# Self-loops of the gate's graph added at the node instead of as edges, and narrower look-ups in the sort

## Chip, cores and metric

One core of a Trainium2 chip runs the whole program, two layers of a graph network, in one launch. The metric is the device time of the launch in microseconds (us).

## What is computed

The reference is two layers over 3125 nodes of 256 values; each has a graph part over 53125 edges, a mixer and an expert layer. The change touches the last expert layer, whose gate is a graph attention over edges of its own: 32768 random pairs between nodes 0 to M-1, M being the number of nodes, and one loop for each node. In the kernel as in the reference (here cut):

```
h = (x_flat @ W_gat).reshape(M, HEADS, NUM_EXPERTS)
loops = jnp.arange(M)
src = concatenate([edge_index[0], loops])
dst = concatenate([edge_index[1], loops])
a_src = (h * att_src).sum(-1)
a_dst = (h * att_dst).sum(-1)
e = leaky_relu(a_src[src] + a_dst[dst], negative_slope=0.2)
e_max = segment_max(e, dst)
ee = exp(e - e_max[dst])
denom = segment_sum(ee, dst)
alpha = ee / (denom[dst] + 1e-16)
agg = segment_sum(h[src] * alpha[:, :, None], dst)
scores = layernorm(agg + b_gat).mean over heads
w = softmax of the two largest of 4 scores
out = sum over experts of w * (gelu(x @ W1 + b1) @ W2 + b2)
```

HEADS is 4 and NUM_EXPERTS 4, so `h` has 16 values a node.

## The kernel before

The program is a row of blocks. In a block each engine has its own list of instructions and waits on semaphores; at its end all engines wait for each other. Nodes stand in 25 blocks of 128. There is no scheduler: what an engine does next is the order written in its function.

**The gate's edges.** They arrive unsorted. `sort_and_route` (L1603) sorts them by destination, for later stages, in the middle of the program. The 32768 pairs fill 256 columns of 128 lanes, the loops 25 more, and 7 columns of fillers bring C2 to 288, 36 turns of U = 8 columns. A destination is split in a low digit (128 values) and a high digit (`so_hi`, NH = 26 values). The **count phase** writes one-hot rows of the low digit (L1912, VectorE) and multiplies them with the high digit's (L1764, TensorE). The **place phase** finds the place of each pair. In one turn: TensorE looks up the start of the pair's node in a table split in two parts (`look`, L1804, in two halves of four matmuls, 52 columns wide: both parts side by side), turns one-hots (`turn_low`, L1782), compares all lanes (`compare`, L1793) and counts equals of lower order (`rank`, L1813, 8 matmuls of 26 columns that add onto the look-ups); VectorE masks the comparison (`order`, L1984), splits the starts (`begin` L1972, `divide` L1977), and in `finish` multiplies the look-ups with the high one-hot (L1988, the pick), reduces (L1993) and casts them (L1995); ScalarE copies (L1867, L1874). In the program's order the first half of a turn's look stands ahead of the compare that the next `order` needs, and waits for the pick of the turn before last, since both use one PSUM tile (`so_g`).

**Scatters.** GpSimd then writes each pair to its place in a table in memory, 128 at a time, one instruction a column (class `Scatter` L2011, L2025), 281 columns. They are spread over stages: 48 in the place phase itself, at most one a turn up to turn 25 and then spread evenly over what is left (`upto_turn`, L1719, each waiting for the turn's cast), beside the routed rows of the first layer's experts; 192 in `experts0` (24 an expert, held back by `pace` to where TensorE is); 16 in `return0`, 25 in `gram1`. `experts0` runs 8 experts: TensorE's two matmul groups (L1465, L1474), a bias on VectorE (L1521) and stores issued by ScalarE (L1497). At the end of `gram1` VectorE works on a row of sums (L2269). 

**The gate.** `build_steps` (in `combine1`) cuts the sorted edges at blocks of nodes: T2 = C2 + NB - 1 = 312 steps, 39 turns. `gate_rows` (L2632) computes 20 values a node, h and a_src, into a table `h_tab`, and a_dst in three bf16 parts in `d_parts`. `gate_scores` (L2817) gathers 128 rows of `h_tab` a step on GpSimd (L2850), ring of four turns; TensorE spreads the destinations (L2889), multiplies the one-hot with `d_parts` (`fetch`, L2899); VectorE reduces the three parts and adds (L2927 to L2932). Behind this TensorE runs the last layer's first experts: each unit a block of nodes by one expert, a hidden half (L2774, `gs_x_h`) and an output half (L2784, `gs_x_y`), 160 such halves' groups spread evenly over the turns, with ScalarE's activation (L2807) and VectorE's bias (L2814) between. `segment_softmax` (L338) turns scores into exponentials of score less the segment's maximum, by scans, in a transposed layout: TensorE transposes into `m2_bank` (L395), VectorE masks (L460) and copies back (L465). Expert blocks run beside it. `gate_sums` (L2959) sums the exponentials and weighted rows by destination: rows cut in three bf16 parts (slices by ScalarE, L3016 and L3017, differences by VectorE, L3040 and L3041), in three chunks of 104 steps, one-hots by VectorE (L3048) and eight matmuls a turn (L3003); 12 expert blocks run between them, and the slices of the next chunk follow ScalarE's activations by the table `SLICED`. `top_two` (L3082) divides, adds the bias, normalises and picks; `experts1` (L3150) runs the rest.

The tile names in rows and orders: `so_` sort, `gs_` scores, `m_` and `m2_` softmax, `gu_` sums, `x_` and `x1_` experts.

## Time and profile before

| | us |
|---|---|
| median of 3 runs | 2887.47 (2885.08 to 2895.32) |
| the profiled execution, its time | 2890.44 |
| its span, first to last instruction | 2888.5 |
| busy TensorE / VectorE / GpSimd / ScalarE | 2220.0 / 1962.4 / 1644.1 / 1402.7 |
| mean granted TensorE clock | .859 |

Each stage's length is set by the engine that ends it. So a total of busy time (TensorE 77%) says little; a stage has to be read by itself, by the busy time of its engines in a stretch of the time axis, and its end by the timeline. In the rows below, PE is TensorE's matmuls, PEld its weight loads, DVE VectorE, ACT ScalarE, POOL GpSimd, SP SyncE; a q behind the name is the engine issuing a DMA. In a row of the timeline the brackets say how long the engine was idle before, and which instruction it waited for.

### The profile page before, as it was taken

The numbers are of one execution on the slowest core, as the hardware profiler recorded it, in microseconds if no ns is written. First come the engines' busy times: TensorE is split into PE (matmuls) and PEld (weight loads), VectorE is DVE, ScalarE is ACT, GpSimd is POOL, SyncE is SP. The second block draws the span as 40 slices with busy tenths as digits, with TensorE's granted clock in tenths as the row PEclk, the third lists the DMA queues.
The fourth block names the chain that finished last, engine by engine and source line by source line (L and its number), as shares of the span: only waits on it lengthen the run. The fifth ranks groups of instructions, "written<-read, shape, count | busy, mean of one in ns | idle before, by whom it ended". The sixth has DMA issues, their size and how long they took to land. (4 is left out here: it accounts for less than half of the span.)

```text
span 2888.5 us, 41571 instructions
## 1 busy us (share of the span) xinstructions
PE 2220.0 (77%) x11092; PEld 1493.3 (52%) x11092; DVE 1962.4 (68%) x4014; ACT 1402.7 (49%) x4464; POOL 1644.1 (57%) x1754
## 2 busy tenths in 40 slices
PE   6996777777777755779974587777787798888785
PEld 3553555555555555656632333333335777777664
DVE  4565999999999888810138799999996322222586
ACT  2221666666666544411133598999994422222242
POOL 2645766666665203567776777777774277777000
PEclk9998888888888855589986799999998699999898
DMA  3214767667665021224322333333331311111005
GB/s 107 57 48 133 212 194 208 201 200 202 201 207 164 1 61 55 66 64 128 99 65 88 87 105 103 104 104 105 103 105 29 73 39 39 31 38 34 14 1 190
DMA packets 170395, 293.24 MB, mean 102 GB/s; under 512 B 56092, under 2 KB 104737, under 8 KB 170174
## 3 DMA queue, kind: packets, MB, share of 16 engines
q0 software_dynamic: 79344, 187.14, 23.8%
q1 hardware_dynamic: 81672, 87.12, 9.7%
q10 hardware_dynamic: 9158, 16.33, 1.6%
q8 instruction: 102, 1.67, 0.2%
q14 instruction: 119, 0.97, 0.1%
HBM read 253.68 MB, written 36.78 MB: 101 GB/s over the span
## 5 line engine op out<-in xcount | busy, mean ns | idle before, releaser
L957 POOL DMA_INDIRECT at_kv<-kv_tab,e_src x440 | 433.8, 986 | 254.0 <-PE at_a L1079 139.1
L2447 PE MATMUL cv_ps<-cv_msg,cv_hot 128*128 128x512 f32 x880 | 421.1, 614 | 125.4 <-DVE acc L2509 83.6
L2434 POOL DMA_INDIRECT cv_x<-x_tab,e_src x440 | 425.6, 967 | 137.3 <-issue 92.3
L2850 POOL DMA_INDIRECT gs_h<-h_tab,fc_q x312 | 294.4, 943 | 161.0 <-issue 93.6
L2465 ACT ACTIVATE cv_msg<-cv_x,factors 128x64 f32<-128x64 f32 x1320 | 357.6, 335 | 0.0
L2025 POOL DMA_INDIRECT pairs<-gating_pair,gating_place x281 | 275.5, 980 | 138.4 <-issue 70.1
L2447 PEld LDWEIGHTS cv_ps<-cv_msg,cv_hot 128*128 128x128 f32 x880 | 158.9, 192 | 349.9 <-ACT cv_msg L2465 177.1
L2509 DVE TENSOR_TENSOR acc<-acc,cv_ps 128x256 f32 x880 | 307.0, 413 | 6.8 <-PE cv_ps L2447 5.2
L1079 PE MATMUL at_a<-at_kv,at_hot_e 128*128 128x264 f32 x880 | 255.6, 420 | 13.4 <-ACT at_hot_e L1006 9.2
L1054 PE MATMUL at_q<-q_parts,at_hot_n 128*128 x1320 | 227.2, 328 | 44.6 <-DVE at_kv L1151 21.9
L2807 ACT ACTIVATE gs_x_hid<-gs_x_h,x_b 128x128 f32<-128x128 f32 x320 | 91.2, 368 | 302.1 <-PE gs_x_h L2774 293.3
L2462 ACT ACTIVATE cv_msg<-cv_x,factors 128x256 f32<-128x256 f32 x440 | 218.3, 496 | 26.2 <-DMA cv_x<-x_tab,e_src 26.1
L2784 PE MATMUL gs_x_y<-x_w,gs_x_hid 128*128 128x256 f32 x640 | 170.0, 416 | 49.6 <-DVE gs_y L2814 49.1
L1054 PEld LDWEIGHTS at_q<-q_parts,at_hot_n 128*128 128x128 bf16 x1320 | 147.0, 113 | 114.6 <-issue 63.5
L1079 PEld LDWEIGHTS at_a<-at_kv,at_hot_e 128*128 128x128 f32 x880 | 165.3, 209 | 48.0 <-ACT at_hot_e L1006 19.2
L1016 ACT ACTIVATE at_kv<-at_kv 128x32 f32<-128x32 f32 x864 | 185.6, 306 | 0.0
L1180 DVE TENSOR_TENSOR acc<-acc,at_a 128x528 f32 x220 | 154.1, 701 | 41.6 <-PE at_a L1079 34.5
L2927 DVE TENSOR_REDUCE gs_as_dst<-gs_d 128x32 f32<-128x96 f32 x39 | 10.0, 258 | 251.6 <-DMA gs_h<-h_tab,fc_q 251.6
L2784 PEld LDWEIGHTS gs_x_y<-x_w,gs_x_hid 128*128 128x128 f32 x640 | 127.4, 208 | 71.3 <-issue 43.7
L2774 PE MATMUL gs_x_h<-xnT,x_w 128*128 128x128 f32 x1280 | 161.6, 283 | 0.0
L2774 PEld LDWEIGHTS gs_x_h<-xnT,x_w 128*128 128x128 f32 x1280 | 158.5, 199 | 2.7
L1151 DVE TENSOR_TENSOR at_kv<-at_kv,at_q 128x512 f32<-128x512 f32 x220 | 147.3, 681 | 14.8 <-DVE at_ends L1253 5.8
(548 smaller groups left out, 4347.2 us busy)
## 6 DMA issues: line engine op xcount, KB each, us to landing
x_space<-in_L_ffn_w SPq DMA_DIRECT2D x16, 1024.0 KB, 6.8
at_rel_row<-e_rel_rows SPq DMA_DIRECT2D x55, 256.0 KB, 4.5
experts_out<-gs_y ACTq DMA_DIRECT2D x20, 512.0 KB, 2.7
x_y<-experts_out SPq DMA_DIRECT2D x20, 512.0 KB, 7.0
at_kv<-kv_tab,e_src POOLq DMA_INDIRECT x440, 3.9
cv_x<-x_tab,e_src POOLq DMA_INDIRECT x440, 2.7
kv_tab<-p_qkv SPq DMA_DIRECT2D x25, 256.0 KB, 2.0
gs_h<-h_tab,fc_q POOLq DMA_INDIRECT x312, 2.4
```

Source lines behind the costliest of these rows:

```text
L957: nc.gpsimd.indirect_dma_start(out=kv[:, t % (RING * Q4), 0:2 * D], out_offset=None, in_=kv_tab, in_offset=bass.IndirectOffsetOnAxis(ap=e. ...
L1054: ins = nc.tensor.matmul(ps_q[dd % 3][:, u, :], hot_n[:, t // Q4 % NHOT, t % Q4 * P:(t % Q4 + 1) * P], q_parts[:, ds(b, 1), n, :].rearrang ...
L1079: nc.tensor.matmul(to, hot_e[:, t // Q4 % NEDGE, t % Q4, :], kv[:, t % (RING * Q4), D:2 * D + H1], start=(u == 0), stop=(u == 1), skip_gro ...
L2025: nc.gpsimd.indirect_dma_start(out=pairs, out_offset=bass.IndirectOffsetOnAxis(ap=place_i[:, c:c + 1], axis=0), in_=pair[:, c, :], in_offs ...
L2434: nc.gpsimd.indirect_dma_start(out=xg[:, i % RT, u, :], out_offset=None, in_=x_tab, in_offset=bass.IndirectOffsetOnAxis(ap=e.src[:, t:t + ...
L2447: nc.tensor.matmul(ps[u % R][:, :], hot[:, i % 2, u, :], msg[:, i % 2, u, :], start=True, stop=True).then_inc(summed, 1)
L2462: nc.scalar.activation(parts[:, 0], xg[:, i % RT, u, :].rearrange("p (r i) -> p r i", i=M), ACT.Copy, scale=factor[:, t:t + 1, 0])
L2465: ins = nc.scalar.activation(parts[:, 1, 1 + m], xg[:, i % RT, u, 0:M], ACT.Copy, scale=factor[:, t:t + 1, 1 + m])
L2509: v.tensor_tensor(row, row, ps[u % R][:, n * D:(n + 1) * D], ALU.add).then_inc(added, 1)
L2774: ins = self.nc.tensor.matmul(self.ps_h[e % 2][:, f * P:(f + 1) * P], self.x1.w1[:, e, c, f * P:(f + 1) * P], self.xnT[:, c, b * P:(b + 1) ...
L2784: ins = self.nc.tensor.matmul(self.ps_y[e % 2][:, 0:D], self.hid[:, e % 2, f, :], self.x1.w2[:, e, f, :], start=(f == 0), stop=(f == FX // ...
L2850: nc.gpsimd.indirect_dma_start(out=hg[:, i % RT, u, :], out_offset=None, in_=h_tab, in_offset=bass.IndirectOffsetOnAxis(ap=e.src[:, i * U ...
```

## The change

The loops are no edges any more. C2 is 256 columns (32 turns), T2 280 (35 turns). The node's own score is computed in `gate_rows` and kept behind a_dst in `d_parts` (24 values a fetch for 12); each edge's score is taken less it. The softmax then takes the larger of the segment's maximum and 0, and gives a second set of values, the exponential of minus that maximum, at the first edge of each segment: the loop's own weight. `gate_sums` adds both (24 columns for 20, 72 a matmul for 60), and `top_two` adds the own term times the node's h. A node with no edge has the weight 1. `gate_rows` keeps h of all blocks. `bank_row` holds the PSUM column where a step's block starts, as 7 blocks of 72 columns fill a bank of 512.

In the sort the two parts of the look-up and the rank are added up in the same 26 columns, so the look is 8 matmuls of 26 columns a half where it was 4 of 52, and the pick and its reduction take 208 elements for 416. The DMA of the fillers and the operations that prepared the loop pairs go. Scatters: 48 in the sort as before, 176 in experts0, 16 in return0, 16 in gram1.

The core of the diff; the pieces, in order, are of the constants, `sort_and_route`, `segment_softmax` (VectorE), `gate_rows`, `gate_scores` (VectorE), `gate_sums` and `top_two`:

```diff
-C2 = (CG + NB + U - 1) // U * U
+C2 = CG
...
-RETURN_SCATTER = C2 // U - 6
+RETURN_SCATTER = C2 // U - 4
...
-                        ins = nc.tensor.matmul(looked(h)[:, u, :, :].rearrange("p a n -> p (a n)"), lo_t[:, h, u, :],
-                                               part[:, h, u, :, :].rearrange("p a n -> p (a n)"), start=(u == 0), stop=False, skip_group_check=True)
+                        for a in range(2):
+                            ins = nc.tensor.matmul(looked(h)[:, u, :], lo_t[:, h, u, :], part[:, h, u, a, :], start=(u == 0 and a == 0),
+                                                   stop=False, skip_group_check=True)
...
-                    v.tensor_tensor(pick[:, :, :, :], looked(i % 2),
-                                    wide(hi[:, i * U:(i + 1) * U, :].unsqueeze(2), [P, U, 2, NH]), ALU.mult).then_inc(picked, 1)
+                    v.tensor_tensor(pick[:, :, :], looked(i % 2), hi[:, i * U:(i + 1) * U, :], ALU.mult).then_inc(picked, 1)
...
+                v.tensor_scalar(b[:, :, :, :], b[:, :, :, :], 0.0, None, ALU.max).then_inc(topped, 1)
+                dve.wait_ge(topped, 1)
                 v.tensor_tensor(x[:, :, :, :], x[:, :, :, :], b[:, :, :, :], ALU.subtract).then_inc(expd, 1)
                 keeps((1, 0), (1, 1))
+                dve.wait_ge(faded, 1)
+                for g in range(groups):
+                    ins = v.scalar_tensor_tensor(out=f[:, g], in0=wide(starts[:, g, :].unsqueeze(1), [P, heads, P]), scalar=0.0, in1=f[:, g],
+                                                 op0=ALU.is_lt, op1=ALU.mult)
+                ins.then_inc(firsts, 1)
                 dve.wait_ge(gone, 1)
...
+                c.link(v.tensor_tensor(own[:, :, :], h[:, :, 16:GW], as_dst[:, :, 0:H2], ALU.add))
+                c.link(v.scalar_tensor_tensor(out=as_dst[:, :, H2:2 * H2], in0=own[:, :, :], scalar=0.2, in1=own[:, :, :],
+                                              op0=ALU.mult, op1=ALU.max))
...
+                    v.tensor_tensor(score[:, i * U:(i + 1) * U, 0:H2], raw[:, :, :], as_dst[:, :, H2:2 * H2], ALU.subtract).then_inc(chain, 1)
...
-    CT = 13
+    CT = 9
-    SLICED = {1: (1, 0), 2: (1, 1), 3: (1, 2), 6: (2, 0), 7: (2, 1), 8: (2, 2)}
-    assert chunks == 3
+    SLICED = {3 * (q - 1) + n: (q, n) for q in range(1, chunks) for n in range(3)}
...
                     q, x = i // CT + 1, i % CT
                     if q < chunks:
-                        if x == 3:
+                        if x == 1:
                             weigh(q)
-                        elif x in (6, 9):
-                            dve.wait_ge(left, 3 * q + x // 3 - 1)
-                            leave(q, x // 3 - 2)
+                        elif x in (3, 6):
+                            dve.wait_ge(left, 3 * q + x // 3)
+                            leave(q, x // 3 - 1)
...
-                c.link(v.tensor_scalar(q[:, 0], acc[:, :, 16:20], 1e-16, None, ALU.add))
+                own, of_edges, total = acc[:, :, 20:24], acc[:, :, 16:20], q[:, 0]
+                c.link(v.tensor_tensor(total, of_edges, own, ALU.add))
+                c.link(v.scalar_tensor_tensor(out=q[:, 2], in0=total, scalar=0.0, in1=own, op0=ALU.is_equal, op1=ALU.add))
+                v.tensor_tensor(t[:, 1].rearrange("p b (h e) -> p b h e", e=NX), h[:, :, 0:16].rearrange("p b (h e) -> p b h e", e=NX),
+                                wide(q[:, 2].unsqueeze(3), [P, NB, H2, NX]), ALU.mult)
+                c.link(v.scalar_tensor_tensor(out=total, in0=q[:, 2], scalar=1e-16, in1=of_edges, op0=ALU.add, op1=ALU.add))
+                c.link(v.tensor_tensor(t[:, 0], acc[:, :, 0:16], t[:, 1], ALU.add))
```

In the place loop, TensorE's list of one turn, before (`so_s` is the comparison, `so_t` the turned one-hots, `so_g` the look-ups and ranks; a number behind the name is the buffer):

```order
L1804 MATMUL so_g1<-so_part,ef_h 128x52 x4
L1782 MATMUL so_t0<-ident_h,x0_space 128x128 x4
L1793 MATMUL so_s1<-ef_h 128x128 x4
L1804 MATMUL so_g1<-so_part,ef_h 128x52 x4
L1782 MATMUL so_t1<-ident_h,x0_space 128x128 x4
L1813 MATMUL so_g0<-so_hi,ef_h 128x26 x8
L1793 MATMUL so_s0<-ef_h 128x128 x4
```

and after:

```order
L1815 MATMUL so_g1<-so_part,ef_h 128x26 x8
L1792 MATMUL so_t0<-ident_h,x0_space 128x128 x4
L1803 MATMUL so_s1<-ef_h 128x128 x4
L1815 MATMUL so_g1<-so_part,ef_h 128x26 x8
L1792 MATMUL so_t1<-ident_h,x0_space 128x128 x4
L1824 MATMUL so_g0<-so_hi,ef_h 128x26 x8
L1803 MATMUL so_s0<-ef_h 128x128 x4
```

The order is the same; each look has 8 narrow matmuls where it had 4.

At the end of the softmax, TensorE's list before (`m2_x` holds the exponentials, `m2_x_h` and `m2_x_y` are an expert's halves):

```order
L395 MATMUL m2_bank0<-ident,m2_x 128x128 x4
L395 MATMUL m2_bank1<-ident,m2_x 128x128 x4
L395 MATMUL m2_bank2<-ident,m2_x 128x128 x4
L2774 MATMUL m2_x_h1<-xnT,x1_w1 128x128 x8
L2784 MATMUL m2_x_y0<-x1_w2,m2_x_hid 128x256 x4
L2784 MATMUL m2_x_y1<-x1_w2,m2_x_hid 128x256 x4
```

and after, with `m2_f` the second set and four banks used in a ring:

```order
L398 MATMUL m2_bank3<-ident,m2_f 128x128 x4
L398 MATMUL m2_bank0<-ident,m2_f 128x128 x4
L398 MATMUL m2_bank1<-ident,m2_f 128x128 x4
L398 MATMUL m2_bank2<-ident,m2_x 128x128 x4
L398 MATMUL m2_bank3<-ident,m2_x 128x128 x4
L398 MATMUL m2_bank0<-ident,m2_x 128x128 x4
L2778 MATMUL m2_x_h1<-xnT,x1_w1 128x128 x8
L2788 MATMUL m2_x_y0<-x1_w2,m2_x_hid 128x256 x4
L2788 MATMUL m2_x_y1<-x1_w2,m2_x_hid 128x256 x4
```

Six groups of transposes stand ahead of the next expert's hidden half where three did.

In `gate_sums`, the end of ScalarE's list before (`gu_part` are slices, `gu_x_hid` an expert's activations):

```order
L2807 ACTIVATE gu_x_hid<-gu_x_h0,x1_b1 128x128 x4
L2807 ACTIVATE gu_x_hid<-gu_x_h1,x1_b1 128x128 x4
L2807 ACTIVATE gu_x_hid<-gu_x_h0,x1_b1 128x128 x4
L3016 ACTIVATE gu_part<-gate_edge_rows 128x104x16
L3017 ACTIVATE gu_part<-score2 128x104x4
L2807 ACTIVATE gu_x_hid<-gu_x_h1,x1_b1 128x128 x4
L3016 ACTIVATE gu_part<-gate_edge_rows 128x104x16
L3017 ACTIVATE gu_part<-score2 128x104x4
L2807 ACTIVATE gu_x_hid<-gu_x_h0,x1_b1 128x128 x4
L3016 ACTIVATE gu_part<-gate_edge_rows 128x104x16
L3017 ACTIVATE gu_part<-score2 128x104x4
L2807 ACTIVATE gu_x_hid<-gu_x_h1,x1_b1 128x128 x4
```

and after:

```order
L3045 ACTIVATE gu_part<-gate_edge_rows 128x72x16
L3046 ACTIVATE gu_part<-score2 128x72x8
L2811 ACTIVATE gu_x_hid<-gu_x_h0,x1_b1 128x128 x4
L3045 ACTIVATE gu_part<-gate_edge_rows 128x64x16
L3046 ACTIVATE gu_part<-score2 128x64x8
L2811 ACTIVATE gu_x_hid<-gu_x_h1,x1_b1 128x128 x4
L3045 ACTIVATE gu_part<-gate_edge_rows 128x64x16
L3046 ACTIVATE gu_part<-score2 128x64x8
L2811 ACTIVATE gu_x_hid<-gu_x_h0,x1_b1 128x128 x4
L3045 ACTIVATE gu_part<-gate_edge_rows 128x64x16
L3046 ACTIVATE gu_part<-score2 128x64x8
L2811 ACTIVATE gu_x_hid<-gu_x_h1,x1_b1 128x128 x4
```

Slices now follow the activations up to the ninth, and the last ones have 64 steps.

## Rows read from the trace of the kernel before

**Rows 1.** busy us of PE, PEld, DVE, ACT, POOL, granted clock, DMA share, GB/s by stretch
```profile
1107.00:1235.00 128.00, 90.50 (x1146) 79.74 (x1144) 108.86 (x214) 60.58 (x130) 69.60 (x72) 0.51 0.23 67
2248.00:2285.00 37.00, 30.75 (x152) 29.84 (x152) 8.81 (x64) 22.42 (x51) 0.00 (x0) 0.50 0.51 125
2285.00:2685.00 400.00, 346.69 (x2304) 294.69 (x2305) 104.04 (x274) 91.89 (x321) 294.35 (x312) 0.92 0.17 35
```

**Rows 2.** the page's groups, the gate's gathers: busy, mean ns, idle before, releaser
```profile
L2850 POOL DMA_INDIRECT gs_h<-h_tab,fc_q x312 | 294.4, 943 | 161.0 <-issue 93.6
```

**Rows 3.** timeline (start, us, engine, line, op), VectorE's work on the loop pairs
```profile
1030.62 0.19 DVE L1898 TENSOR_TENSOR so_loop<-so_loop,node_mask 128x25 f32<-128x25 f32 x1
```

**Rows 4.** timeline, VectorE in the count phase
```profile
1081.16 9.16 DVE L1912 TENSOR_TENSOR x_space<-so_count_h,so_digit 128x1024 bf16<-128x1024 bf16 x8
```

**Rows 5.** timeline, two turns of the place loop
```profile
1221.84 1.22 DVE L1984 TENSOR_TENSOR ef_h<-so_s,so_not_before 128x1024 bf16<-128x1024 f32 x1 [0.34 <-PE so_s L1793]
...
1222.13 0.41 PE L1813 MATMUL so_g<-so_hi,ef_h 128*128 128x26 bf16 x8
...
1223.27 0.58 DVE L1988 TENSOR_TENSOR so_last<-so_g,so_hi 128x416 f32<-128x416 f32 x1
...
1224.00 0.33 PE L1804 MATMUL so_g<-so_part,ef_h 128*128 128x52 bf16 x4 [0.93 <-DVE so_last L1988]
...
1224.59 0.37 DVE L1972 TENSOR_TENSOR so_start<-so_upto,so_flag 128x208 f32<-128x208 f32 x1
...
1225.29 1.23 DVE L1984 TENSOR_TENSOR ef_h<-so_s,so_not_before 128x1024 bf16<-128x1024 f32 x1 [0.34 <-PE so_s L1793]
```

**Rows 6.** timeline, the end of the sort: VectorE's casts, GpSimd's last scatter, the next block
```profile
1230.69 0.17 DVE L1995 CAST gating_place<-so_place 128x8 int32<-128x8 f32 x1
...
1232.01 0.17 DVE L1995 CAST gating_place<-so_place 128x8 int32<-128x8 f32 x1
...
1233.66 0.96 POOL L2025 DMA_INDIRECT pairs<-gating_pair,gating_place  x1 [0.30 <-issue]
...
1236.36 2.15 SPq L1425 DMA_DIRECT2D x_rows<-expert_rows  x4
```

**Rows 7.** timeline, the end of experts0; and the page's DMA issues
```profile
1477.26 1.82 ACTq L1497 DMA_DIRECT2D expert_out<-x_y  x4
...
1489.55 0.95 POOL L2025 DMA_INDIRECT pairs<-gating_pair,gating_place  x1 [0.30 <-issue]
...
experts_out<-gs_y ACTq DMA_DIRECT2D x20, 512.0 KB, 2.7
```

**Rows 8.** timeline, the end of gram1 and VectorE's start of the next block
```profile
1602.11 0.41 DVE L2269 COPY sums<-g_row 1x256 f32<-1x256 f32 x1 [0.69 <-PE g_row L2231]
...
1607.39 0.96 POOL L2025 DMA_INDIRECT pairs<-gating_pair,gating_place  x1 [0.30 <-issue]
...
1611.35 0.06 DVE L2303 MEMSET np_n<- 1x1 f32 x1 [8.82 <-PEq L2167]
```

**Rows 9.** TensorE's groups in gate_scores, and a stretch of it as in rows 1
```profile
L2784 PE MATMUL gs_x_y<-x_w,gs_x_hid 128*128 128x256 f32 x634 | 167.5, 414 | 49.6 <-DVE gs_y L2814 49.1 <-ACT gs_x_hid L2807 0.5
...
L2889 PE MATMUL gs_b<-gs_rel_row,ones_h 1*128 1x512 bf16 x78 | 25.4, 408 | 8.5 <-DMA x_b<-in_L_ffn_b 7.0 <-DVE gs_hot L2919 1.5
...
2345.00:2365.00 20.00, 20.00 (x144) 17.52 (x144) 5.36 (x14) 4.64 (x17) 15.12 (x17) 1.00 0.18 35
```

**Rows 10.** timeline, VectorE's masks at the softmax's end
```profile
2731.45 1.89 DVE L460 TENSOR_TENSOR m_x<-m_x,e_hole 128x512 f32<-128x512 f32 x3
```

**Rows 11.** TensorE's sums as a group, and a difference of VectorE's in the timeline
```profile
L3003 PE MATMUL gu_ps<-gu_part,gu_hot 128*128 128x60 bf16 x312 | 28.0, 197 | 15.9 <-ACT gu_part L3017 8.8 <-issue 5.6 <-DVE gu_hot L3048 1.3
...
2747.14 1.89 DVE L3040 TENSOR_TENSOR gate_edge_rows<-gate_edge_rows,gu_part 128x1664 f32<-128x1664 f32 x1 [1.04 <-ACT gu_part L3017]
```

**Rows 12.** timeline, two `order`s early in the place loop
```profile
1111.92 1.23 DVE L1984 TENSOR_TENSOR ef_h<-so_s,so_not_before 128x1024 bf16<-128x1024 f32 x1 [1.02 <-PE so_s L1793]
...
1114.95 1.22 DVE L1984 TENSOR_TENSOR ef_h<-so_s,so_not_before 128x1024 bf16<-128x1024 f32 x1
```

More of the change, by code:

```diff
@@ L39 @@
 H2 = 4
-assert T1 % U == 0 and T2 % U == 0
+assert T1 % U == 0 and T2 % U == 0 and C2 % U == 0
 B5 = 5
@@ L2956, in _, with bank_at, gate_sums @@
                 dve.wait_ge(freed, turns)
[L2959 to L2962 removed]
+def bank_at(b):
+    return b * 3 * ROWW + b // BANKED * (512 - BANKED * 3 * ROWW)
+def gate_sums(nc, k, e, rows, weight, acc, x1, xnT, bank_row):
+    W = ROWW
+    W3 = 3 * W
     turns = T2 // U
[L2964 removed]
+    CT = 9
     CS = CT * U
[L2966 to L2967 removed]
+    chunks = -(-turns // CT)
+    assert SUMS * 8 < turns and NB <= 4 * BANKED
     PER = SUMS * 8 / turns
[L2969 to L2970 removed]
+    SLICED = {3 * (q - 1) + n: (q, n) for q in range(1, chunks) for n in range(3)}
+    assert len(SLICED) <= SUMS * NX
     POS = {2: 0, 4: 1, 6: 2, 7: 3}
@@ L2998, in _ @@
                 for i in range(turns):
-                    blocks = blocks_of(nc, mybir.EngineType.PE, e, i)
+                    starts = nc.values_load_multi_w_load_instructions(
+                        bank_row[0:1, ds(i * U, U)], engines=(mybir.EngineType.PE,), min_val=0, max_val=bank_at(NB - 1),
+                        skip_runtime_bounds_check_because="bank_row holds bank_at of a block, which build_steps clamps to 0..NB-1")[1]
                     pe.wait_ge(cut, 3 * (i // CT) + 3)
                     pe.wait_ge(built, i + 1)
-                    for u, b in enumerate(blocks):
-                        ins = nc.tensor.matmul(ps.rearrange("p q w -> p (q w)")[:, ds(b * W3, 3 * W)], hot[:, i % 4, u, :],
+                    for u, at in enumerate(starts):
+                        ins = nc.tensor.matmul(ps.rearrange("p q w -> p (q w)")[:, ds(at, W3)], hot[:, i % 4, u, :],
                                                part[:, i // CT % 2, i % CT * U + u].rearrange("p n w -> p (n w)"),
```

166 lines of the change are left out of this document (88 added, 78 removed).

## The prediction

> **What bounds the kernel now.** I read three views: the busy time of each engine in stretches, the groups by line, and the timeline at the ends of the stages. The profiled execution took 2890.44 us (span 2888.5); the median of three runs is 2887.47. My sum is a difference, made in the profiled execution and subtracted from the median. The kernel is a row of stages, each a block in which all engines wait for the last one, so an edit is worth what it takes off the engine that ends its stage.
>
> [...] In gate_scores GpSimd issues 312 gathers of .943 us and is idle 93.6 us for plain issue [rows 2], .30 us before each, as before its scatters [rows 6]: 1.25 us a gather with few exceptions, 390 of the stage's 400 us. TensorE is busy 347 there, so it stands close behind. In experts0 and gram1 GpSimd ends last, with scatters (below).
>
> **The change, part by part.** Turns of eight columns go from 36 to 32 in the sort and from 39 to 35 in the gate; 281 scatters become 256.
>
> *Loop pairs.* Seven small VectorE operations of about .19 us [rows 3] go: -1.4.
>
> *Count phase.* Eight one-hot writes take 9.16 us [rows 4], 1.145 a turn, and TensorE waits for each. Four turns: -4.6, and with the shorter high-digit writes **-5.0** (-4.5 to -5.5).
>
> *Place loop.* One turn, in the order in which things are released [rows 5]: `order` from 1221.84 (1.22 us), the divide, the pick from 1223.27 (.58); it ends at 1223.85, TensorE's next look starts at 1224.00, its turn and compare follow, and the next `order` starts at 1225.29, 3.45 us behind the first. The pick's reduction and cast and `begin` lie in the 1.44 us in which VectorE waits for that chain (`order` still waits .34 us behind them), so the halved reduction is worth nothing. Four turns fewer: **-13.8**. The pick itself halves from 416 to 208 elements: by `begin` on 208 it takes .37 instead of .58, -.21 a turn. Against it, the look in front of the compare becomes eight matmuls of 26 columns instead of four of 52. The four take .33 us, the eight of the same width in `rank` .41: +.08, at the same columns. Bounds: nothing, since the columns are the same, and .16 if each of the four added costs what one of `rank` does (.05) with the second look too slow to hide. Net -.13 to -.21 at best, -.05 at worst; I take -.05 a turn with the larger price, since the path starts with the look: -1.6 over 32 turns (0 to -6.7).
> [...]
>
> *The scatters' tail.* GpSimd scatters 48 columns during the sort, one a turn up to turn 25 and the other 23 spread over what is left: 11 turns before, 7 after. Now the last two casts stand at 1230.69 and 1232.01, 1.3 us apart, the last scatter ends at 1234.62, 2.4 us behind, and the next block starts at 1236.36, 1.7 later [rows 6]. After, 23 scatters at 1.26 us are 29.0 us from turn 25 on, and the turns give 6 x 3.4 + 1.3 = 21.7: the last one ends 7.6 us behind the last cast. **+5.2** (+3 to +7), a new wait.
>
> *experts0.* It gets 176 scatters instead of 192. Now the last ends at 1490.50 [rows 7], while ScalarE's last stores are issued by 1479.08. With 22 an expert, GpSimd needs 27.7 us, where 24 take 30.3. In eight experts it falls 13 us behind TensorE, whose last result is stored from 1477.26; eight times 2.5 us is more than that, so it no longer does, and the stage ends with the stores: 1479.08 and 2.7 us for a store of ScalarE's to land (the row of the gate's stores, the nearest [rows 7]), 1481.8. That is 8.7 earlier; I take **-8** (-6.5 to -9.5), with the edge for the block's end. return0 keeps its 16.
>
> *gram1.* 16 scatters instead of 25. Now the last ends at 1608.35 and the next block starts at 1611.35; VectorE's last copy ends at 1602.51 [rows 8]. Nine scatters are 11.3 us, so GpSimd would end at 1597 and VectorE is next: 1602.5 plus the 1.7 us of a block's end is 1604.2, **-7.2** (-5 if the end costs 3.0 as behind GpSimd, -8).
>
> *gate_rows.* VectorE gets two small operations and rows twice as wide; it is busy 8.8 of 37 us there [rows 1], and SyncE's loads end the stage: 0 (up to +1).
>
> *gate_scores.* 32 gathers fewer: 32 x 1.25 = -40 if GpSimd stays the bound. Behind it stands TensorE: 347 us busy in the stage, of which the spread of the rows (25.4 us in 39 turns, .65 a turn [rows 9]) loses four turns and the experts' units lose nothing; the fetch keeps its count a turn with 24 columns for 12. That leaves 344 us of work beside GpSimd's 353. The stretch from 2345 to 2365 shows that TensorE can be busy 20.0 us of 20 [rows 9]. It is a near draw, so GpSimd's waits for freed slots should grow somewhat; the ring of four turns evens most of them out. I take **-35** (-40 to -23).
>
> *Softmax.* A maximum with 0, a second exponential, three masks of 128x512 and twelve more transposes. The three masks of x take 1.89 us [rows 10]; three more stand ahead of them, behind the wait for an expert's block, which hides the maximum. The copies double, but TensorE transposes beside them, and behind its last transposes stand experts 13 to 15, which end the stage; so its transposes' delay counts, the masks and a wait of some .6 us for a bank. **+2.5** (+1.5 if half of the masks is hidden by the wait for the expert's block, +5 if the three added copies, by size above the masks, end the stage).
>
> *gate_sums.* TensorE ends it. A turn's eight matmuls are .72 us busy (28.0 in 39 turns) and .14 of issue in front [rows 11]: four turns fewer are -3.4, and the first chunk's slices and differences are 72 columns, not 104: by size, from 1.89 us for a difference on 104 columns [rows 11] and slices about as long, three of each in a row before the first turn, -2.3 of what would be 3 or more. Against it: 72 instead of 60 columns a matmul, +.7; four short reductions, +.4; and on ScalarE a slice now stands behind every activation from 0 to 8, each waiting for the weighing of its chunk, so that experts' units wait for it: at turn 19 about 2.6 us, at turn 7 1.0. Sum **-1.0** (-5 to +3).
>
> *top_two.* Four more VectorE operations in the one chain, on 400 and 100 elements; a tile of 208 takes .37 us [rows 5] and one of 25 .19 [rows 3], so about .2 and .6 each: **+1.8** (1 to 3). experts1 shifts with it.
>
> Sum: -1.4 - 5.0 - 13.8 - 1.6 + 5.2 - 8 - 7.2 - 35 + 2.5 - 1.0 + 1.8 = -63.5, so 2887.5 - 63.5 = **2824.0 us**.
>
> **The rivals.**
> [...] Chance .09.
> [...]
> *TensorE becomes the bound of gate_scores.* Its work per turn grows by a ninth (4.57 expert units instead of 4.10), and every pause for VectorE (49.6 us before the output matmuls) is then lost. 344 busy and a third of those pauses kept give 360 to 385; at 377 the stage gains 23 instead of 35: 2836. For it: TensorE's share would be .97 of GpSimd's time. Against: before its gathers GpSimd was idle 161.0 us in all, of which 93.6 is issue [rows 2]; in the stretch of rows 9 with TensorE full it kept its pace (15.1 of 20 us, as issue allows). Chance .17.
> *The stages stay as long as they were*, because something not seen (stores, DMA queues) holds them: 2887. In gate_scores the DMA share is .17, nothing speaks for it. Chance .01.
> *Slower than before.* In gate_scores TensorE's clock falls to the lower level. Of its 2304 matmuls in 39 turns, 59 a turn, the full-clock stretch from 2345 to 2365 has 144, so a turn's work is 8.2 us there [rows 9], the stage's 320, and after the change 317; at the lower level it is at most twice that. [...] Against: the stretches with TensorE busiest had the clock at 1.00. Chance .01.
> My forecast: .72.
>
> **How the numbers follow.** The unknown costs add to -12 and +16 around 2824 if half of them fall the same way; the clock case lies at 2811 and the TensorE-bound case at 2836. 2806 to 2842 holds about .85. A measurement of this kernel tells some .5% (14 us) from no change; faster than 2873 are the forecast and both neighbours: .97, within .5% .015, slower .015.
>
> **What would show it.** In the profile after: two `order`s 3.40 us apart (3.45 or more: the look costs what the pick gains; 3.0: the clock rose); the last scatter 7 to 8 us behind the last cast; experts0 ending with ScalarE's stores and gram1 with VectorE; 280 gathers of .94 us, with GpSimd idle for plain issue before nearly all, and a stage of about 365; if TensorE bounds it, GpSimd's idle time names TensorE's matmuls. The softmax and top_two longer by 2 us each. What would make me wrong is gate_scores above all: it carries over half of the sum.

## The result

The changed kernel takes 2806.66 us (2806.19 to 2807.19, four runs), the kernel before 2889.15 beside it: ratio .9704, interval .9687 to .9722, 82.5 us less. Forecast were 63.5 less, at most 81.5. The direction was right and the gain was larger, by a microsecond more than the range allowed: 2806.66 itself stands inside 2806 to 2842, but the range was put down beside 2887.5 for the kernel before. A second group of runs of both kernels gave 2810.54 beside 2896.86, 86.3 less. One run of the kernel before in that second group, 3680.06 us at a mean granted clock of .546 where the ten others have .854 to .861, is left out of the ratios.

By stage, from the same rows of both traces (from the start of the stage's first such instruction to the next one's; `pairs<-r_rows` is the first, and stands 1.2 us later in the trace after, which is why the changes add up to 85.1 and the profiles differ by 84.0):

| stage | before | after | change | forecast |
|---|---|---|---|---|
| loop pairs and count phase, to the first `order` | 81.6 | 74.8 | -6.8 | -6.4 |
| place loop, to the last cast | 122.9 | 103.8 | -19.1 | -15.4 |
| last cast to experts0 | 4.4 | 11.4 | +7.1 | +5.2 |
| experts0, to return0's first gather | 256.5 | 246.1 | -10.3 | -8 |
| return0 and gram1, to VectorE's last copy | 109.3 | 108.4 | -.8 | 0 |
| end of gram1 | 9.8 | 1.7 | -8.2 | -7.2 |
| convolve, combine1, gate_rows | 673.1 | 671.3 | -1.8 | 0 |
| gate_scores, first to last gather | 394.5 | 350.2 | -44.3 | |
| gate_scores, behind the last gather | 12.1 | 9.7 | -2.4 | -35 with the row above |
| softmax | 51.3 | 51.1 | -.2 | +2.5 |
| gate_sums, to top_two's block | 91.2 | 89.2 | -2.0 | -1.0 |
| top_two, to its first reciprocal | .3 | 2.0 | +1.7 | +1.8 |
| the rest, to the end | 54.0 | 55.9 | +2.0 | 0 |

Where the forecast had a sign, the stage has it too, but for the softmax. The last row's 55.9 is this one profile's: all thirteen others have 53.1 to 54.3 us there.

### The profile page after: what moved, and what is told of

It reads as the page before. It is cut to its first block and busy times, and to the rows that moved or that the text cites. A ratio compares the mean times of both kernels' runs of the same rounds, so it can differ in the third digit from the quotient of the medians.

```text
span 2804.5 us, 41419 instructions
## 1 busy us (share of the span) xinstructions
PE 2188.2 (78%) x11127; PEld 1471.0 (52%) x11128; DVE 1941.9 (69%) x4018; ACT 1399.9 (50%) x4455; POOL 1587.4 (57%) x1697
## 5 line engine op out<-in xcount | busy, mean ns | idle before, releaser
L2857 POOL DMA_INDIRECT gs_h<-h_tab,fc_q x280 | 264.5, 945 | 147.2 <-issue 79.2
L2025 POOL DMA_INDIRECT pairs<-gating_pair,gating_place x256 | 251.8, 984 | 125.7 <-issue 64.7
L2811 ACT ACTIVATE gs_x_hid<-gs_x_h,x_b 128x128 f32<-128x128 f32 x320 | 91.5, 368 | 260.5 <-PE gs_x_h L2778 260.5
L2788 PE MATMUL gs_x_y<-x_w,gs_x_hid 128*128 128x256 f32 x640 | 154.9, 388 | 27.5 <-DVE gs_y L2818 26.3
L1015 ACT ACTIVATE at_away_e<-count_row,e_rel 128x128 f32<-128x128 f32 x440 | 139.8, 388 | 17.6 <-PEq L864 15.8
L1508 ACT ACTIVATE x_hid<-x_h,x_b 128x489 f32<-128x489 f32 x64 | 42.8, 669 | 200.1 <-PE x_h L1479 200.1
```

Source lines behind the costliest of these rows:

```text
L2025: nc.gpsimd.indirect_dma_start(out=pairs, out_offset=bass.IndirectOffsetOnAxis(ap=place_i[:, c:c + 1], axis=0), in_=pair[:, c, :], in_offs ...
L2857: nc.gpsimd.indirect_dma_start(out=hg[:, i % RT, u, :], out_offset=None, in_=h_tab, in_offset=bass.IndirectOffsetOnAxis(ap=e.src[:, i * U ...
```

## The profile after

Busy time by stretch (as rows 1): the place loop, and gate_scores.

```profile
1102.50:1208.00 105.50, 81.64 (x1265) 72.15 (x1261) 82.84 (x189) 54.09 (x115) 63.24 (x65) 0.52 0.27 81
...
2246.30:2602.00 355.70, 325.46 (x2269) 282.14 (x2270) 111.50 (x299) 92.14 (x321) 264.54 (x280) 0.97 0.17 38
```

The traces show TensorE's granted clock at two levels, 1.00 (rows 9) and .50 (the kernel before from 1221.84 to 1225.29). The place loop is at the lower one nearly throughout (mean .52), as before (.51 in rows 1); in gate_scores the mean is .97 where rows 1 have .92, and TensorE is busy 325.5 us where they have 346.7.

The place loop's timeline; to set beside rows 5:

```profile
1195.08 1.22 DVE L1985 TENSOR_TENSOR ef_h<-so_s,so_not_before 128x1024 bf16<-128x1024 f32 x1 [0.59 <-PE so_s L1803]
...
1196.50 0.37 DVE L1989 TENSOR_TENSOR so_last<-so_g,so_hi 128x208 f32<-128x208 f32 x1
...
1197.02 0.37 PE L1815 MATMUL so_g<-so_part,ef_h 128*128 128x26 bf16 x8 [0.77 <-DVE so_last L1989]
...
1198.35 1.23 DVE L1985 TENSOR_TENSOR ef_h<-so_s,so_not_before 128x1024 bf16<-128x1024 f32 x1 [0.59 <-PE so_s L1803]
```

From `order` to `order` are 3.27 us, before 3.45. The pick is .37 for .58. The look (8 matmuls, .37) starts .15 behind the pick's end as before, and from the pick's end (1196.87) to the next `order` 1.48 us pass, before 1.44: the narrow look costs .04 and the narrow pick gives .21.

The end of the sort, as rows 6:

```profile
1206.46 0.17 DVE L1995 CAST gating_place<-so_place 128x8 int32<-128x8 f32 x1
...
1207.35 0.17 DVE L1995 CAST gating_place<-so_place 128x8 int32<-128x8 f32 x1
...
1216.09 0.96 POOL L2025 DMA_INDIRECT pairs<-gating_pair,gating_place  x1 [0.30 <-issue]
...
1218.79 1.77 SPq L1439 DMA_DIRECT2D x_rows<-expert_rows  x4
```

The last scatter ends at 1217.05, 9.5 us behind the last cast's end, with no wait in front of it.

The ends of experts0 and gram1, as rows 7 and 8; the first line, the start of the block behind experts0, is of the kernel before:

```profile
1492.11 0.10 POOL L1561 MEMSET re_top<- 128x1 f32 x1 [1.61 <-POOLq L1417]
...
1459.23 0.96 POOL L2025 DMA_INDIRECT pairs<-gating_pair,gating_place  x1 [0.30 <-issue]
...
1460.38 1.83 ACTq L1511 DMA_DIRECT2D expert_out<-x_y  x4
...
1464.21 0.10 POOL L1575 MEMSET re_top<- 128x1 f32 x1 [4.02 <-POOLq L1431]
...
1567.71 0.96 POOL L2025 DMA_INDIRECT pairs<-gating_pair,gating_place  x1 [0.30 <-issue]
...
1573.37 0.41 DVE L2269 COPY sums<-g_row 1x256 f32<-1x256 f32 x1 [0.69 <-PE g_row L2231]
...
1574.45 0.06 DVE L2303 MEMSET np_n<- 1x1 f32 x1 [0.67 <-PEq L2167]
```

GpSimd is done before the stores are issued (1462.21), and the next block starts 2.0 us behind them. In gram1 the next block starts .67 us behind VectorE's copy.

The gathers as a group, as rows 2:

```profile
L2857 POOL DMA_INDIRECT gs_h<-h_tab,fc_q x280 | 264.5, 945 | 147.2 <-issue 79.2 <-POOLq L2649 60.7 <-PE gs_x_y L2788 4.6
```

Of the 147.2 us idle 60.7 are the wait for the stage, 79.2 plain issue and 4.6 waits for TensorE's output halves. As the experiments show, the last come from a hold: every second gather of GpSimd waits until TensorE's experts have come as far in their list as the gathers in theirs.

The end of the stage: TensorE's last output half, before and after.

```profile
2684.22 3.75 PE L2784 MATMUL gs_x_y<-x_w,gs_x_hid 128*128 128x256 f32 x8 [4.67 <-DVE gs_y L2814]
...
2600.54 1.97 PE L2788 MATMUL gs_x_y<-x_w,gs_x_hid 128*128 128x256 f32 x8 [1.00 <-DVE gs_y L2818]
```

The end of the softmax; the first line is of the kernel before:

```profile
2731.11 0.42 DVE L2814 TENSOR_TENSOR x_late<-m_x_y,x_b 128x256 f32<-128x256 f32 x1 [3.09 <-PE m_x_y L2784]
...
2644.26 0.42 DVE L2818 TENSOR_TENSOR x_late<-m_x_y,x_b 128x256 f32<-128x256 f32 x1 [0.93 <-PE m_x_y L2788]
...
2644.61 1.89 DVE L468 SCALAR_TENSOR_TENSOR m_f<-e_rel,m_f 128x512 f32<-128x512 f32 x3
...
2646.41 1.89 DVE L473 TENSOR_TENSOR m_x<-m_x,e_hole 128x512 f32<-128x512 f32 x3
...
2646.55 1.29 PEld L398 LDWEIGHTS m_bank<-ident,m_f 128*128 128x128 f32 x12 [2.72 <-DVE m_f L468]
...
2648.21 2.02 DVE L478 COPY score<-m_bank 128x512 f32<-128x512 f32 x2
```

VectorE's wait for an expert's block in front of the masks is .93 us, before 3.09. The masks of the second set (L468) stand from 2644.61 and x's (L473) behind them, 40.2 us behind the stage's first transposes, where before they stood 39.8 behind (2731.45 in rows 10, the transposes at 2691.66). TensorE's transposes run at the upper level (granted clock 1.00 from 2646 to 2656).

gate_sums, the two places where TensorE waits:

```profile
2683.24 0.76 DVE L3070 TENSOR_TENSOR score<-score,gu_part 128x576 f32<-128x576 f32 x1
...
2685.67 1.12 ACT L2811 ACTIVATE gu_x_hid<-gu_x_h,x_b 128x128 f32<-128x128 f32 x4
...
2686.85 3.58 PE L2788 MATMUL gu_x_y<-x_w,gu_x_hid 128*128 128x256 f32 x8 [3.42 <-ACT gu_x_hid L2811]
...
2710.16 1.22 DVE L3064 TENSOR_TENSOR gate_edge_rows<-gate_edge_rows,score 128x1024 f32<-128x1024 f32 x1
...
2714.07 3.49 PE L2788 MATMUL gu_x_y<-x_w,gu_x_hid 128*128 128x256 f32 x8 [2.94 <-ACT gu_x_hid L2811]
```

Each time the output half waits for the expert's activation (L2811), which ScalarE has behind a slice that is not ready. The first time the slice is the second chunk's last, which waits for VectorE's difference (L3070); the second time it is the fourth chunk's first, which waits for its weighing (L3064 at 2710.16; its 1024 elements are 64 steps). Both waits are followed by matmuls at the lower level (granted clock .54 and .56), 3.58 and 3.49 us where others take 1.97.

## Experiments

Each kernel's time is a median of at least four runs, and its ratio is to the kernel before, run on the same chip: that kernel's medians were 2890.2, 2896.9 and 2891.5 in the three groups. The changed kernel was in the second group. Stages are read from each kernel's own profile, which is of one run and not always of one near the median. One run's stages differ from another's where the code is the same: in the fourteen profiles the place loop has one interval of 5.0 to 5.8 us near its start four times, and convolve to gate_rows goes from 670.8 to 683.0 us. So medians that are some microseconds apart are weak evidence here, and the readings rest on the stages.

**Wide look.** Back to 52 columns and 416 elements, at 32 turns:

```diff
...
-                        for a in range(2):
-                            ins = nc.tensor.matmul(looked(h)[:, u, :], lo_t[:, h, u, :], part[:, h, u, a, :], ...)
+                        ins = nc.tensor.matmul(looked(h)[:, u, :, :].rearrange("p a n -> p (a n)"), lo_t[:, h, u, :],
+                                               part[:, h, u, :, :].rearrange("p a n -> p (a n)"), ...)
...
```

> The changed kernel with the look-up of the sort as before: four matmuls of 52 columns, pick and reduction of 416 elements. In the changed kernel two orders stand 3.27 us apart where the kernel before had 3.45. Theory (the narrow pick gives .21 a turn, the eight narrow matmuls of the look cost .04): orders 3.44 to 3.46 apart, the last order later by 31 x .17 = 5.3 us, but the stage only by some 4.3, since in its last seven turns GpSimd's 23 scatters set the end either way; whole kernel 2811. Rival (the shorter turn comes from something else, as memory traffic or fewer turns): orders stay 3.27 apart and the time at 2806.7. As the prediction priced it (.05 a turn): orders 3.32 apart, 2808.

2815.67 us, ratio .974 (.9705 to .9775). Two orders of its timeline:

```profile
1197.61 1.22 DVE L1984 TENSOR_TENSOR ef_h<-so_s,so_not_before 128x1024 bf16<-128x1024 f32 x1 [0.33 <-PE so_s L1803]
...
1201.05 1.22 DVE L1984 TENSOR_TENSOR ef_h<-so_s,so_not_before 128x1024 bf16<-128x1024 f32 x1 [0.34 <-PE so_s L1803]
```

3.44 apart, the last one 5.4 us later against the first than in the changed kernel. The tail behind the last cast is 9.7 us instead of 11.4, so of the 6.2 us that the loop takes longer to its last cast, the next stage starts 4.5 later. So the edit is worth .17 us a turn. The median is 4.7 above the expected 2811. The profiled run is the longest of the four (2825.47): its gathers took 359.1 us and convolve with gate_rows 683.0, neither of which the edit touches. How much of that is in the other three runs is not known.

**40 columns in the sort.**

```diff
-SORT_SCATTER = 6
+SORT_SCATTER = 5
...
-                    pool.wait_ge(scatter.sent[h], 16 * U * (scatter.turns // 2))
+                    pool.wait_ge(scatter.sent[h], 16 * U * ((scatter.turns + 1 - h) // 2))
...
-        assert self.turns % 2 == 0
```

> The changed kernel with 40 of the 256 columns scattered in the sort instead of 48; experts0 gets 184 instead of 176, 23 an expert. Theory (the tail behind the last cast is the 23 scatters that are left over after turn 25, 1.26 us each): 15 of them take 18.9 us in seven turns that take over 20, so the last one ends 1.5 to 3 us behind the last cast instead of 9.7, and the stage ends 7 to 8 us earlier; experts0 needs 29.0 us of GpSimd an expert beside 28.2 of TensorE and ends later by 0 to 6. Whole kernel 2799 to 2804. Rival (the end of the sort waits for rows or for the tables of the routing, not for scatters): the stage ends where it did and the kernel takes 2807 to 2812.

2808.68 us, ratio .9729 (.9688 to .9771). Its end of the sort:

```profile
1208.73 0.17 DVE L1995 CAST gating_place<-so_place 128x8 int32<-128x8 f32 x1
...
1210.82 0.96 POOL L2024 DMA_INDIRECT pairs<-gating_pair,gating_place  x1 [0.30 <-issue]
...
1213.48 1.77 SPq L1439 DMA_DIRECT2D x_rows<-expert_rows  x4
```

4.8 us from the last cast to experts0, not 11.4; experts0 takes 245.9 us beside 246.1, and return0 with gram1 1.4 more than in the changed kernel's profile. The tail is the scatters. The median misses the expected 2799 to 2804 and does not show the 6.7 us; this kernel's runs spread over 16 us. The stages show it, and the combined kernels below. Some of it is given back. In the four kernels with 40 columns experts0 takes 245.9 to 248.0 us, in three of them with the last scatter ending behind the last store again, where the eight other changed ones have 245.1 to 247.8; and return0 with gram1 takes 109.8 to 110.3 where those have 107.8 to 109.1, for a reason that was not looked for.

**Earlier weighing.**

```diff
-                        if x == 1:
+                        if x == 1 and q == 1:
                             weigh(q)
...
+                        elif x == 7 and q + 1 < chunks:
+                            weigh(q + 1)
```

> The changed kernel with the weighing of the third and fourth chunk of gate_sums moved from the second turn of the chunk before to two turns earlier (VectorE's list only). Theory (in the changed kernel TensorE waits 3.42 and 2.94 us for an expert's activation that stands on ScalarE behind the slice of a chunk not yet weighed, and each wait is followed by a group of matmuls at the lower clock, 3.5 us for 2.0): both waits go, the stage takes 81 to 84 us instead of 89.2, whole kernel 2798 to 2801. Rival (TensorE's work sets the stage and the waits only move it): less than 2 us, 2805 to 2807.

2803.96 us, ratio .9707 (.9668 to .9747). gate_sums takes 83.4 us instead of 89.2, inside the expected 81 to 84; the median, with a spread of 10.5 us, is above the expected 2798 to 2801 and its ratio is that of the changed kernel. TensorE's output halves as a group, and the wait that is left:

```profile
L2788 PE MATMUL gu_x_y<-x_w,gu_x_hid 128*128 128x256 f32 x96 | 27.0, 431 | 3.6 <-ACT gu_x_hid L2811 3.4
...
2693.55 3.53 PE L2788 MATMUL gu_x_y<-x_w,gu_x_hid 128*128 128x256 f32 x8 [3.42 <-ACT gu_x_hid L2811]
```

In the changed kernel the same group waits 8.6 us, 8.5 of it for ScalarE: .94, 2.94 and 1.19 besides the 3.42 of the first. The edit takes those three away, and the slow group behind the 2.94. The first wait stays, as it stands behind a difference and not behind a weighing, so the theory that both go was half right. What was moved is worth 5.8 us; the waits on ScalarE that I had foreseen were 3.6 in all.

**More work for TensorE in gate_scores.**

```diff
-                    for n in range(0, U * P, 512):
+                    for n in list(range(0, U * P, 512)) * 2:
```

> The changed kernel with the spread of the rows in gate_scores done twice on TensorE (four matmuls of 512 columns a turn instead of two, the same result): about .62 us a turn more, 22 us in 35 turns, so TensorE has 347 us of work beside GpSimd's 350. Theory A (GpSimd bounds the stage, TensorE has what is left of each turn, and more work keeps its clock up): the gathers stay 1.255 us apart and the stage longer by at most 3 us; kernel 2806 to 2810. Theory B (the stage is a near draw and each microsecond of TensorE's comes out, as the prediction's rival had it): stage longer by 10 us or more, kernel over 2815.

2815.55 us, ratio .9736 (.9699 to .9774). The spread takes 39.5 us instead of 21.8, the gathers 362.2. From the first gather to the last the mean granted clock is .95, in the seven profiles with the hold and without the added work .94 to .97: more work did not raise it. The gathers' time looks like theory B, but the kernel with the wide look had 359.1 with no work added. All gaps of up to 1.30 us between gathers have the same mean in every profile but two (1.251), 1.248 or 1.249. In the changed kernels the rest is a few of up to 2.2 us in the first 22 us, and up to five of 1.4 to 5.3 us, at about 59, 130, 204, 274 and 347 us behind the first gather: every 56 gathers, seven turns, in which exactly 32 units stand (4.57 a turn). The changed kernel's first profile has only the first two of them.

**The changed kernel again.**

> The changed kernel itself, once more, beside the others of this group. Of the five profiles so far of this or a nearly equal gate_scores, the time from its first gather to its last was 350.2, 359.1, 353.0, 354.6 and (with more TensorE work) 362.3 us, while all gaps between gathers under 1.30 us had the same mean, 1.248 to 1.249. Theory (the rest are single waits of 1 to 4 us that come back every 56 gathers, seven turns, where 32 expert units end together with a whole number of turns): 350 to 359 us again, with the long gaps at 59, 130, 204, 274 and 347 us behind the first. Rival (my first reading, that the changed kernel's gathers run without waits and are 350 us): 350 to 351.

2810.54 us, ratio .9699 (.9677 to .972). Gathers 359.5 us, with gaps at 59, 132, 203, 274 and 346. My first reading, that these gathers run without waits, fell: the 350.2 of the first profile had 1.8 us of excess gaps, this one 11.2. With the profiles of the five other kernels that have the hold and the same work in gate_scores (352.8 to 359.1) the mean of the seven is 354.7, 39.8 less than before. The last gap in the timeline:

```profile
2594.48 0.29 PEld L2906 LDWEIGHTS gs_d<-d_parts,gs_hot 128*128 128x128 bf16 x8 [0.84 <-issue]
...
2595.81 0.94 POOL L2857 DMA_INDIRECT gs_h<-h_tab,fc_q  x1 [0.30 <-issue]
...
2595.78 0.75 DVE L2818 TENSOR_TENSOR gs_y<-gs_x_y,x_b 128x256 f32<-128x256 f32 x2
...
2596.35 3.47 PE L2788 MATMUL gs_x_y<-x_w,gs_x_hid 128*128 128x256 f32 x8 [1.48 <-DVE gs_y L2818]
...
2599.89 0.36 DVE L2934 TENSOR_REDUCE gs_as_dst<-gs_d 128x64 f32<-128x192 f32 x1 [3.35 <-DMA gs_h<-h_tab,fc_q]
...
2600.57 0.96 POOL L2857 DMA_INDIRECT gs_h<-h_tab,fc_q  x1 [3.82 <-PE gs_x_y L2788]
```

TensorE's output half (L2788) waits for VectorE's bias and then runs at the lower clock (granted .56 from 2596.35 to 2599.82, 3.47 us); GpSimd's next gather waits for that output, 3.82 us.

**No hold on the gathers.**

```diff
-                        if i and u % 2 == 0:
-                            x = upto(i - 1) + (upto(i) - upto(i - 1)) * u // U
-                            run.passed(pool, x // 8, x % 8)
```

> The changed kernel without the wait that holds each second gather of gate_scores back to where TensorE's expert units are; the ring of four turns alone holds GpSimd. Theory (the long gaps are a ring of waits: VectorE's list has the reduction that waits for gathers ahead of the bias that frees TensorE's output bank, TensorE's output waits for it, and GpSimd's next gather waits for that output): the gaps named PE go, first to last gather 348.5 to 351 us in the profile, and the kernel is 2 to 8 us faster than the changed one beside it. Rival (the gaps are TensorE's own lack of time, so GpSimd only waits elsewhere, for the ring): 352 to 360 us, the waits now put down to VectorE's copy.

2806.22 us, ratio .9689 (.967 to .9709), 4.3 less than the changed kernel beside it. Gathers 348.5 us, one gap of 1.42:

```profile
L2854 POOL DMA_INDIRECT gs_h<-h_tab,fc_q x280 | 264.4, 944 | 145.8 <-issue 85.0 <-POOLq L2649 60.8
```

Idle for issue is 85.0 us, and TensorE is not named. So the floor from the first gather to the last is 279 x 1.248, 348.2 us. In gaps of over 1.30 us the four kernels without the hold lose .2 to .4 us and the eight changed ones with it 1.8 to 13.7: what is lost in such gaps comes through the hold. The medians alone would not show it, as the two kernels' runs overlap (2805.07 to 2808.46 beside 2806.59 to 2815.95).

**The kernel before at the changed density.**

```diff
-            return round(EARLY * 8 * i / turns)
+            return min(EARLY * 8, round(EARLY * 8 * i / 35))
...
+                            x = min(x, EARLY * 8 - 1)
```

> The kernel before (312 gathers) with the expert units of gate_scores spread over the first 35 turns instead of 39: 4.57 a turn, the changed kernel's density. Theory (the changed kernel's gate_scores was 46.8 us shorter because of 32 gathers at 1.25, 40.0, and 6.9 us of chance and of the stage's end, not because of a granted clock raised by density): first to last gather 390 to 399 us (before 394.5), the end of the stage behind the last gather 2 to 4 us shorter, as no unit is left there; kernel within 0.3% of before. Rival (density keeps the clock up and removes GpSimd's waits): first to last gather 388 to 390.

2880.43 us, ratio .9961 (.9939 to .9982). Gathers 394.5 us, the same as before, though now with gaps at 60, 130, 201, 272 and 343: density moves the waits and does not remove them, and the mean granted clock from the first gather to the last is .92 as before. Behind the last gather are 4.7 us instead of 12.1, and the softmax takes 48.2 instead of 51.3 (the expectations count the softmax from a point 2.4 us later than the table here). That is more than the 2 to 4 us that I had expected, and so the kernel is .4% faster where I had expected a change of at most .3%.

**The first two edits together.**

> The changed kernel with 40 columns scattered in the sort (as in the second experiment) and the earlier weighing (as in the third). Their gains by stage in those profiles were 6.1 us (sort and experts0 together) and 5.8 us (gate_sums), in stages that share nothing. Theory: they add up to 11.9, some 2795 where the changed kernel has 2807. Rival (a later stage gives one of them back): 6 or less.

2800.95 us, ratio .9671 (.9652 to .969), 9.6 less than the changed kernel beside it, where 11.9 had been expected; no run of the one is as slow as the fastest of the other. The sort's end takes 4.8 us and gate_sums 82.9; return0 with gram1 takes 110.3, beside 109.1 in the changed kernel of this group, and the place loop has one of the long intervals (5.47).

**Three edits.**

> The changed kernel with three edits: 40 columns scattered in the sort, the earlier weighing, and no hold on GpSimd's gathers. By stage their gains were 6.1, 5.8 and (gathers 348.5 instead of 350.2 to 359.5) 2 to 11 us. Theory: they are in different stages and add up, 2793 to 2797 where the changed kernel had 2807 to 2811. Rival (the freed gathers or scatters take time from a later stage): 2800 or more.

The third is the missing hold. 2795.9 us, ratio .9654 (.9625 to .9682), inside the expected 2793 to 2797. Gathers 349.4, sort's end 4.8, gate_sums 83.4.

**Three edits, and no unit in the last turn.**

The units of gate_scores are spread over 34 of its 35 turns.

> The kernel with the three edits and, in gate_scores, the 160 expert units spread over the first 34 of the 35 turns (4.71 a turn instead of 4.57). With 35 of 39 turns in the kernel before, the gathers took the same 394.5 us, and the stage's end behind the last gather went from 14.5 to 7.0 us, the softmax from 49.0 to 45.9. Theory (the end of the stage is expert units that TensorE still has to do behind the last gather): gathers 348.5 to 350, end 7 to 9 us instead of 12, kernel 3 to 6 us faster than the one with three edits. Rival (TensorE has no room left at 9.9 us of gathers a turn): gathers 352 or more, no gain.

2790.86 us, ratio .9637 (.961 to .9665). Gathers 348.5; the end of the stage:

```profile
2597.57 0.42 DVE L2817 TENSOR_TENSOR gs_y<-gs_x_y,x_b 128x256 f32<-128x256 f32 x1 [1.30 <-PE gs_x_y L2787]
...
2598.61 0.94 POOL L2853 DMA_INDIRECT gs_h<-h_tab,fc_q  x1 [0.30 <-issue]
...
2602.26 0.19 DVE L2938 TENSOR_TENSOR score<-gs_raw,gs_as_dst 128x32 f32<-128x32 f32 x1
...
2603.05 2.80 PE L368 MATMUL m_bank<-ident,score 128*128 128x128 f32 x12 [5.33 <-PEq L2846]
```

TensorE's first transposes start 4.4 us behind the start of the last gather, 11.5 in the kernel above. The softmax gives back 1.2. By its median it is the fastest kernel of the study, 5.0 below the one above. The two kernels' runs overlap, and their profiled runs took the same (2796.98 and 2797.1), as this one's convolve with gate_rows took 6.5 us longer.

**Softmax without the second set.** It leaves out the set's exponential, masks, transposes and copies, so the loops' weights are 0 in it.

```diff
-                for at, (ready, data) in enumerate(((firsts, f), (final, x))):
+                for at, (ready, data) in enumerate(((final, x),)):
...
```

> The changed kernel's softmax without the second set of values: its exponential, three masks, twelve transposes and three copies are left out (the loops' own weights are 0 then, so the output is not the reference's); the maximum with 0 stays. In the changed kernel softmax took 48.7 us from TensorE's first transposes to VectorE's first work of the next stage, before 49.0, where +2.5 had been forecast. Theory (VectorE waited 3 us for an expert's block there before, so the second set fills a wait): without it the stage is 47 to 49 us, so the set costs 0 to 1.5. Rival (it costs its 2.5 us and something else became faster): 45.5 to 46.5.

2807.44 us, ratio .9694 (.9666 to .9722). The softmax takes 50.3 us; with the set 51.1 in the changed kernel's first profile and 50.5 in its second, 50.5 to 51.2 in all profiles with unchanged gate_scores. So the set costs .2 to .9 us.

**More work, no hold.**

> The changed kernel without the hold on the gathers and with the spread of the rows done twice on TensorE (22 us of work more in the stage). With the hold the double spread gave 362.3 us from first to last gather; without it the single spread gave 348.5. Theory (the hold turned passing lateness of TensorE into waits of GpSimd; by work TensorE has just enough room): 348.5 to 352 us, the end of the stage behind it up to 3 us longer. Rival (TensorE's work is the bound at that load): 358 to 365 us as with the hold.

2812.45 us, ratio .9724 (.9677 to .977), spread over 2801.7 to 2824.4. The profiled run took 2804.5, with gathers of 349.2 us:

```profile
L2854 POOL DMA_INDIRECT gs_h<-h_tab,fc_q x280 | 265.1, 947 | 146.5 <-issue 85.1 <-POOLq L2649 61.4
...
L2893 PE MATMUL gs_b<-gs_rel_row,ones_h 1*128 1x512 bf16 x140 | 37.8, 390 | 8.1 <-DMA gs_rel_row<-e_rel_rows 6.6 <-DVE gs_hot L2923 1.5
```

The spread takes 37.8 us, without the hold and the added work 22.3. So in this run TensorE had room for 15.5 us more; with the hold, the same work gave 362.2. Two of the four runs took 2820 us and more and have no profile, so whether they lost it here is not known.

## Why the prediction was short

*What bounds the kernel* was right, and so were the signs of the stages but for the softmax. The terms were mis-sized, and one step of the argument failed.

*gate_scores, -35, measured -46.7 in the profiles: the step that failed.* The rows gave -40 for a bound by GpSimd, and I moved it to -35 because TensorE's 344 us of work made it a near draw. There was no draw. TensorE was busy 325.5 us at a granted clock of .97 (334.8 at .94 in the second profile). The 344 had been taken from 346.7 us of busy time at .92, some of it matmuls at the lower level; the 317 us that the prediction itself works out for the slow rival was the better measure. The 353 us beside it was too large too: 280 x 1.25 are 350, and from the first gather to the last are 348.2. And in the profiled run without the hold TensorE took 15.5 us more without moving a gather. With the hold as it is, work added beyond the change's may still cost: 17.7 us more gave 362.2, above all seven profiles without it (350.2 to 359.5). What GpSimd loses above 1.248 a gather goes through the hold: 6.3 us before and on average of the seven profiles, but 1.8 in the changed kernel's first and 11.2 in its second. So of the 46.7 us 39.9 are the 32 gathers, 4.5 chance of that profile and 2.4 the stage's end. Over the two profiles of the changed kernel the gathers were 44.3 and 35.0 us shorter, over all seven 39.8.
The stage's end behind the last gather was left out of the prediction. TensorE's last output group took 1.97 us there instead of 3.75, the upper clock for the lower (granted 1.00 for .50), behind a wait of 1.00 us instead of 4.67. What makes the clock fall at such a wait was not tried.

*The place loop, -1.6 besides the four turns, measured -5.3.* I had taken the look's larger price, .16 a turn, because it opens the path. The row gave .08, and the timeline shows .04. The look's eight narrow matmuls take .37 us, its four wide ones took .33. The wide look showed the .17 a turn by itself.

*The ends.* experts0 gave 10.3 instead of 8. The sum counted from the last scatter's end (1490.50), but the stage before ended 1.6 us later, with the next block's start at 1492.11; and that start comes 2.0 us behind the last store's issue, sooner than the 2.7 taken for its landing. The tail of the sort cost 7.1 instead of 5.2: the turns were 3.27 us and not 3.40, the last two casts stood .9 apart and not 1.3, and two of the 23 scatters took 1.15 us. That makes 1.6 of the 1.9; the second experiment showed the tail to be scatters. gram1 was right to 1 us, which is the block's end: .67 us behind VectorE's copy and not 1.7.

*The softmax, +2.5, measured -.2.* The price stood on the masks lying behind VectorE's wait for an expert's block. The maximum and the masks fill that wait (3.09 us before, .93 after), so x's masks stand only .4 us later, and the kernel without the set is .2 to .9 us faster there. *gate_sums, -1.0, measured -2.0*, with a path that was mis-sized: the two waits on ScalarE were foreseen at 1.0 and 2.6 us, and were 3.4 and 2.9 with a slow group behind each, so the rest of the sum gave more than forecast; what of it did was not taken apart. *top_two, +1.8*, was 1.7.

*The rivals.* The prediction's 2811, the clock case, is the place loop with all `order`s 3.03 us apart, as rows 12 have two at a mean granted clock of .92 (1111.92 to 1114.95). No run shows that over the whole loop: it stayed at .52 with `order`s 3.27 apart. Nor does a profile have gate_scores at the lower level, the case at the far end: its mean there, from the first gather to the last, is .92 to .97 in all fourteen profiles. TensorE as the bound of gate_scores did not come; one profile with the hold lost 11.2 us of the gathers' gain by the hold. Nothing became slower but the sort's tail and top_two's start.

What stays open: the stage of convolve, whose code is the same in all, took 638.6 to 650.6 us in these profiles to the first table row of gate_rows. That spread is as large as most terms here, and was not looked into. Nor were the long interval in four of the place loops, and the 1.7 us that return0 with gram1 takes longer on average with 40 columns in the sort.

## What to carry over

When one engine paces another by hand, so that it does not run ahead, price the stage twice: by the sum of its work and with every passing lateness turned into a wait. In this case the hold's cost came back with the period at which the two lists line up, and went from 1.8 to 11.2 us between two profiles of one kernel.
A term that removes work from the engine that ends a stage should be taken at its full price, with the new bound as a rival of its own, not averaged between. And where work is taken off a stage whose leftovers are spread over its last turns, look at what piles up behind the last one: 23 scatters in seven turns cost 6.7 us that 15 did not, of which later stages gave some back.

## What was not expected of the hardware

From one gather's start to the next, where nothing is waited for, are 1.248 or 1.249 us in every profile but two (1.251), with TensorE busy 86% (the kernel before at the changed density) to 95% of the time (more work, no hold); what differs between runs is single waits. Some waits of TensorE are paid twice: a group of eight output matmuls took 3.3 to 3.8 us behind them instead of 2.0 (granted clock .50 to .58 instead of 1.00). A wait's length alone does not tell which. Of 159 such groups in the fourteen traces that follow a wait of 1.4 to 3 us, 68 took up to 2.1 us and 44 took 3.3 or more.
